# A fourth pair of PSUM banks is divided between the value products and the turned tiles

## The reference

```
scores = einsum('bhqd,bhkd->bhqk', q, k) / sqrt(HD)
scores = where(causal, -inf, scores)          # layer 0 only
attn_w = softmax(scores, axis=-1)
attn   = einsum('bhqk,bhkd->bhqd', attn_w, v)
```

## Time and profile before

| | |
|---|---|
| Median of 3 runs | 1529.98 us (1524.67 to 1530.46) |
| Profiled execution, own time | 1526.45 us |
| Its span | 1524.7 us |
| TensorE (products) busy | 1369.9 us, 90% |
| VectorE busy | 1249.3 us, 82% |
| ScalarE busy | 1081.6 us, 71% |
| GpSimd busy | 278.1 us, 18% |
| Mean granted TensorE clock | 0.97 of full speed |

### The profile page before, as it was taken

One profiled execution on the slowest core, in us unless ns is written; L12 is line 12 of the kernel. 1 busy time (PEld: TensorE's weight loads), 2 busy tenths in 40 slices (PEclk: granted clock), 3 DMA queues, 4 the chain that ended last, 5 costly groups with the idle time before them and its releaser, 6 DMA issues.

```text
span 1524.7 us, 31977 instructions
## 1 busy us (share of the span) xinstructions
PE 1369.9 (90%) x13016; PEld 565.3 (37%) x13016; DVE 1249.3 (82%) x1715; ACT 1081.6 (71%) x1239; POOL 278.1 (18%) x624
## 2 busy tenths in 40 slices
PE   6699999999998768888679999999999999999886
PEld 3333434343343334446423333233333333233355
DVE  7978888888885387885989999999999999997143
ACT  6167777777777657764358888888888888887642
POOL 4021322223133132332200000000000000001252
PEclk9689999999999899999889999999999999999998
DMA  5610110101100000012120000000000000000001
GB/s 177 168 45 24 31 38 25 45 24 42 27 4 3 1 1 0 1 65 82 42 64 23 23 24 23 14 17 18 23 23 23 23 23 23 3 3 3 1 15 42
DMA packets 38995, 47.90 MB, mean 31 GB/s; under 512 B 11072, under 2 KB 20160, under 8 KB 38720
## 3 DMA queue, kind: packets, MB, share of 16 engines
q1 hardware_dynamic: 38416, 45.31, 10.1%
q10 hardware_dynamic: 432, 0.53, 0.1%
HBM read 30.22 MB, written 15.47 MB: 30 GB/s over the span
## 4 chain that ended last, share of the span: by engine, by line
PE 62%; DVE 23%; ACT 6%; issue 4%; POOL 3%; SPq 1%; DMA 1%; POOLq 0%; ACTq 0%; DVEq 0%
PE ps L426 22%; DVE l_negp L324 14%; PE ps L404 12%; PE ps L383 12%; PE ps L552 7%; ACT shared L296 3%; PE ps L443 2%; PE ps L389 2%; POOL n_rs L514 2%; DVE n_bst L495 2%; PE ps L545 1%; PE ps L1040 1%; SPq L113 1%; PE ps L908 1%; PE ps L560 1%
## 5 line engine op out<-in xcount | busy, mean ns | idle before, releaser
L324 DVE TENSOR_REDUCE l_negp<-ps 128x2 f32<-128x1024 f32 (+2 forms) x832 | 953.3, 1181 | 75.5 <-PE ps L389 36.4
L296 ACT ACTIVATE shared<-ps 128x1024 f32<-128x1024 f32 (+1 forms) x832 | 820.4, 991 | 196.8 <-PE ps L404 168.1
L426 PE MATMUL ps<-shared,l_vs 128*32 128x256 f32 (+3 forms) x6648 | 515.3, 386 | 4.1 <-POOL shared L280 3.3
L383 PE MATMUL ps<-Ks,Qs 48*128 48x512 bf16 (+3 forms) x1792 | 329.9, 369 | 40.6 <-DVE l_negp L324 27.2
L404 PE MATMUL ps<-Qs,Ks 51*128 51x512 bf16 (+3 forms) x1792 | 320.8, 366 | 25.5 <-ACT shared L296 10.7
L404 PEld LDWEIGHTS ps<-Qs,Ks 51*128 51x128 bf16 x1792 | 81.3, 93 | 330.6 <-issue 159.3
L426 PEld LDWEIGHTS ps<-shared,l_vs 128*32 128x32 f32 x6648 | 134.8, 108 | 172.3 <-issue 141.7
L383 PEld LDWEIGHTS ps<-Ks,Qs 48*128 48x128 bf16 x1792 | 87.6, 94 | 194.3 <-ACT shared L296 91.0
L280 POOL TENSOR_SCALAR_AFFINE_SELECT shared<-shared 128x512 f32<-128x512 f32 x128 | 81.7, 639 | 321.0 <-ACT shared L296 320.9
L265 POOL CAST l_parts<-l_negm 128x16 bf16<-128x16 f32 x64 | 12.6, 197 | 441.8 <-DVE l_negm L329 438.6
L389 PE MATMUL ps<-mask,id 64*128 64x128 bf16 x1024 | 69.2, 223 | 0.0
(11 more groups left out here) (160 smaller groups left out, 1090.4 us busy)
## 6 DMA issues: line engine op xcount, KB each, us to landing
Qs<-scr_q SPq DMA_DIRECT2D x128, 64.0 KB
Ks<-scr_k SPq DMA_DIRECT2D x64, 96.0 KB
Qs<-scr_q SPq DMA_DIRECT2D x128, 32.0 KB
Ks<-scr_k SPq DMA_DIRECT2D x64, 64.0 KB
scr_q<-own SPq DMA_DIRECT2D x4, 768.0 KB, 3.6
scr_q<-shared SPq DMA_DIRECT2D x4, 768.0 KB, 3.5
scr_k<-own SPq DMA_DIRECT2D x4, 768.0 KB, 5.0
scr_k<-shared SPq DMA_DIRECT2D x4, 768.0 KB, 4.8
```

The source lines that it names most:

```text
L296: act.activation(dst, src, ACT.Exp, scale=SCALE).then_inc(exped, 1)
L324: dve.tensor_reduce(dst, src, AX_X, ALU.max, negate=True).then_inc(reduced, 1)
L383: last = pe.matmul(outs[par], Qs[s][r:r + MROW, h2, qt * P:(qt + 1) * P], Ks[s][r:r + MROW, h2, at:at + w], start=True, stop=True)
L426: last = pe.matmul(pv_ps[q % 2][32 * h:32 * h + 32, a:a + wide], vs[g % 2][:, kt, h, :], pT[m % PRING][:, h, a:a + wide], start=m == u.fir ...
```

## The change

The value products of every half group go to bank 6. Bank 7 becomes a place of its own for turn_max and turn_out, one behind the other, which therefore no longer take part in the ring; only while a stage holds pair 3 do they still take the ring's next pair. The first W of each half group waits for the copy of the half group directly before it. The copy (evacuate) is put one tick earlier, at the last key unit's tick + 2 in place of + 3 counted from the end of its keys.

```diff
-                    (self.k_ends[q] + 3, ("evacuate", q)), (self.k_ends[q] + 4, ("turn_out", q))]
+                    (self.k_ends[q] + 2, ("evacuate", q)), (self.k_ends[q] + 4, ("turn_out", q))]
...
-    pv_ps = [ps[:, (6 + i) * BANK:(7 + i) * BANK] for i in range(2)]
+    pv_ps = ps[:, 6 * BANK:7 * BANK]
 
     def slot(entry):
         n = place.slot[entry]
+        if n == RING:
+            return ps[:, 7 * BANK:8 * BANK].unsqueeze(1)
         return ps[:, 2 * n * BANK:(2 * n + 2) * BANK].rearrange("p (two c) -> p two c", two=2)
...
-            act.activation(outT[:, :], pv_ps[q % 2], ACT.Copy).then_inc(evacuated, 1)
+            act.activation(outT[:, :], pv_ps, ACT.Copy).then_inc(evacuated, 1)
...
-                    if q % NPER < 2:
+                    if q % NPER == 0:
                         pe.wait_ge(handed.v_made[g // NGRP], B)
-                    if q >= 2:
-                        pe.wait_ge(evacuated, q - 1)
+                    if q:
+                        pe.wait_ge(evacuated, q)
...
-                last = pe.matmul(pv_ps[q % 2][32 * h:32 * h + 32, a:a + wide], vs[g % 2][:, kt, h, :],
+                last = pe.matmul(pv_ps[32 * h:32 * h + 32, a:a + wide], vs[g % 2][:, kt, h, :],
...
+            elif entry[0] in ("turn_max", "turn_out") and RING not in held:
+                self.slot[entry], self.before[entry] = RING, had[RING]
+                had[RING] = entry
             elif entry[0] in ("key", "max", "turn_max", "turn_out"):
```

## The result

The changed kernel takes 1514.38 us, the median of 15 runs (1512.04 to 1524.45), against 1527.56 of the kernel before in as many (1522.59 to 1533.39). The ratio is 0.9915, with a 95% interval of 0.990 to 0.993: faster by 13 us. Its profiled execution has a span of 1512.0 us, 12.7 less than that before.

What follows compares the result with a forecast made beforehand. Layer 1 was taken to be set by a loop through PSUM slots, not a full engine. Gains of 4.2 us in layer 1 and 8.6 in layer 0, together 13, took 1526.45 to 1513 us; forecast's own range 1506 to 1518.

Steps and rivals of the forecast that it cites:

- Maxima leave the ring: At turned row maxima, K and M no longer wait for a shifted slot: 0.42 us gained per layer 1 half group.
- the two places: Layer 0's two turned maxima per group: the M behind each follows its K sooner, gaining 0.58 and 0.27 us.
- Turned outputs: Turned outputs in layer 1 cost only their own TensorE time before and after, so leaving the slots gains nothing.
- One bank: Between half groups, first W waits for the copy: 0.28 us lost in layer 1 and short to long, zero long to short.
- W's own delay: First W of a half group waits for the copy's end and a 0.06 us hop, so comes 0.17 us late.
- the border that was to cost zero: Layer 0, long to short half: next K waits for VectorE anyway, so W may be 0.25 us late for nothing.
- Sum: Both attentions: 4.2 us less in layer 1 and 8.6 in layer 0, together 13 us, giving 1513 us.
- The prediction's claim that nothing outside the regular ticks changes: Stages between and behind the attentions: they hold no changed instruction, so nothing was counted there.
- a free border: Rival, between half groups: copy is done when W wants it, slack absorbs ScalarE's loss; 25.4 us less, 1501; chance 0.10.
- the border eats the gain: Rival: each change of half group costs about 0.4 us on the mean, time stays at 1526; chance 0.24.
- left the turned tiles in the ring: Rival: slots run as before, only the new wait stays; 13 us more, 1539; both slower rivals together 0.11.
- The slower one, the open copy: Rival: each half group waits out the copy, 0.75 or 0.40 us; 15 us more, 1541; both slower rivals together 0.11.

Runs made afterwards that it cites:

- the kernel that has the gain alone: Against the kernel before: value products alternate between two banks, copy at its old tick, turned tiles use whichever bank was last copied out; 1501.63 us, ratio 0.9816.

## Why the prediction was right, step by step

The forecast was 1513 us, the measured median 1514.38, and the terms can be checked one by one. The forecast started from the profiled execution's 1526.45 us; the median of 15 runs before, 1527.56, lies closer to it than to the 1529.98 of three, from which 1517 would have come.

*Maxima leave the ring:* 0.42 us per half group of layer 1 and 0.85 per group of layer 0 were worked out; the kernel that has the gain alone shows 0.44 and 0.88. In layer 0 the two places can be told apart by the steps from copy to copy: 0.27 and 0.58 were worked out, 0.28 (18.08 to 17.80 us) and 0.60 (8.70 to 8.10) came. The way in which it comes is that of the rows: M follows K by 0.22 to 0.23, and of VectorE's gap under 0.1 is left.

*Turned outputs:* counted at nothing; the kernel without that part has the same steps to a hundredth or two.

*One bank:* 0.28 us at a border of layer 1 and from short to long half, zero from long to short. The difference between the changed kernel and the one with two banks is 0.27 per half group of layer 1 and 0.30 per group of layer 0. Of the latter, 0.29 stand in the step with the border from short to long half (17.80 to 18.09 us) and 0.01 in the other (8.10 to 8.11), as forecast. One piece under it was mis-sized: W's own delay was put at 0.17, from a hop of 0.06 behind the copy's end, and is 0.26, from a hop of 0.15. It changed nothing, because the exponential pushed by 0.28 held the next M as long as that. At the border that was to cost zero, W may be 0.25 late for nothing, so there the error used up the slack and no more; that this held is luck.

*Sum:* 15 x 0.58 + 30 x 0.17 is 13.8 us against 12.8 worked out. The profiled executions, counted by turned outputs, show what the sum left out. Layer 0 is 9.0 us shorter from its first to its last one, and layer 1 is 5.0 shorter up to the last three half groups; these are what the sum counts. Ahead of layer 0's first turned output another 2.2 us are gained, the stage between the layers is 1.5 longer, and the end of layer 1 is 2.1 longer, where the border met the layer norm on ScalarE and the clock fell. These nearly cancel, so that the total came out within 2 us is in part luck. The prediction's claim that nothing outside the regular ticks changes was its weakest step.

*The rivals:* a free border would have been the 1501 us of the kernel with two banks, which had no border to pay. The one in which the border eats the gain needed 0.30 to 0.54 us per border on the mean; 0.27 in layer 1, 0.29 and 0.01 in layer 0 came. The one that left the turned tiles in the ring was put at 1539 and measured 1541. The slower one, the open copy, was put at 1541, with a loss of up to 0.75 us at a border. With the copy one exponential later the time was 1631: W waits for longer, 1.22 to 1.31, and TensorE's clock, which the price left out, fell behind many of them. On the rule of the Trainium skill, Perfetto Trace Analysis, "Matmuls", that independent groups of products should rotate through banks: the runs here agree with it, with 13 us between the kernel that rotates and the one that doesn't, though the change that broke the rule was still a gain over the one that followed it with a shared ring.

## What to carry to other kernels

Where every engine is near full, look for the loop that closes through buffers before naming a bound: here the time of two ticks was a loop of K, its exponential, M and W, and taking two fifths of VectorE's work in layer 1 away left the half group at 20.12 us. A rare user of a small ring costs more than its own time, because it exchanges what its neighbours wait for; give it a place that is idle at that moment before taking one away from somebody. When a double buffer is given up, what counts is how far the copy is from the engine's queue head: one place later in ScalarE's order made a gain of 13 us a loss of 102.

## What the runs showed of the hardware

TensorE's granted clock fell to its lower level behind some waits of 1.2 to 2.5 us, and not behind others of the same length: 0.52 over 202.0 to 205.4 us after a wait of 1.22 (copy at its old tick), where 6 of the 21 such waits left it up; 0.52 over 1402 to 1409 after one of 2.46 (changed kernel), and 1.00 over the same stretch after one of 2.46 in the kernel with only the maxima out of the ring. Eight products that ran at the lower level took 1.08 us in place of 0.64. The waits of 0.19 us at the changed kernel's regular borders left the clock at 1.00. What decides between these cases is not shown here.

From the end of ScalarE's copy to the first product that waited for it there were 0.15 us (1018.47 to 1018.62), where from the end of an exponential to the weight load of the M that waited for it there were 0.05 to 0.06 (1018.36 + 1.03 to 1019.44 in the changed kernel).
